# Attention scores on row tiles, with both images of a pair issued together

## The reference

```python
t = t + _L2_attn_ref(_ln_t(t), ...)   # 8 heads of 16, causal window of 64 keys
t = t + _L2_ffn_ref(_ln_t(t), ...)    # y = x @ binarized weight + bias; y = round(clip(y, -1, 1) * 7) / 7
t = t + _L3_attn_ref(_ln_t(t), ...)   # 8 heads of 16, causal
t = t + _L3_ffn_ref(_ln_t(t), ...)    # 8 experts, the best two of softmax(x @ W_router)
# each attention: scores = q @ k.T / 4; masked softmax; out = probs @ v; out @ W_o
```

## Time and profile before

| | |
|---|---|
| median of 3 runs | 270.75 us (270.49 to 271.74) |
| profiled execution, its own time | 271.7 us |
| its span, first to last instruction | 269.9 us |
| granted TensorE clock over the span | 1.000 |
| busy PE, DVE, ACT, POOL | 93%, 79%, 64%, 31% |
| phases of attention | 43.6 to 71.6, to 105.3, to 138.6, to 171.8 |
| experts | from 171.8 |

### The profile page before, as it was taken

How to read it: one execution, slowest core, us unless ns; L and a number is a source line. 1 busy time by engine, 2 the same in 40 slices (tenths; PEclk the granted TensorE clock), 3 DMA queues, 4 the chain that set the end, 5 groups by cost and what they waited for, 6 DMA issues and landing times.

```text
span 269.9 us, 4613 instructions
## 1 busy us (share of the span) xinstructions
PE 251.7 (93%) x1545; PEld 184.6 (68%) x1547; DVE 212.7 (79%) x542; ACT 172.6 (64%) x490; POOL 83.8 (31%) x151
## 2 busy tenths in 40 slices
PE   7999879699998998989999899999899999999994
PEld 2777557465776566666576666788678878888883
DVE  3675669965599797997979957397699969599985
ACT  2276344698676856768667697675485587567760
POOL 5100104988894762946724220000400000000000
PEclk9999999999999999999999999999999999999999
DMA  7800000014222020000000000041101000531101
GB/s 219 323 2 2 0 1 0 0 29 130 80 78 79 8 73 2 0 2 0 0 5 0 0 2 2 24 134 43 38 32 47 2 0 0 170 99 48 39 0 39
DMA packets 9318, 11.84 MB, mean 44 GB/s; under 512 B 704, under 2 KB 5952, under 8 KB 9168
## 3 DMA queue, kind: packets, MB, share of 16 engines
q1 hardware_dynamic: 8864, 11.23, 13.7%
q10 hardware_dynamic: 432, 0.33, 0.4%
HBM read 11.00 MB, written 0.56 MB: 43 GB/s over the span
## 4 chain that ended last, share of the span: by engine, by line
PE 57%; DVE 30%; ACT 6%; issue 4%; POOL 2%; DMA 1%; DVEq 0%; SPq 0%; ACTq 0%
PE bank L717 5%; PE bank L729 5%; PE bank L693 5%; PE bank L665 5%; DVE negmax L1083 5%; PE bank L959 4%; PE bank L960 4%; PE bank L962 4%; PE bank L947 4%; PE bank L949 3%; PE bank L948 3%; DVE probT L1142 3%; DVE hlo L1337 2%; DVE ht L1049 2%; DVE stats L1035 2%
## 5 line engine op out<-in xcount | busy, mean ns | idle before, releaser
L479 ACT ACTIVATE prob<-bank,negmax 128x256 f32<-128x256 f32 (+1 forms) x128 | 52.5, 425 | 17.1 <-DVE negmax L1083 16.7
L606 ACT ACTIVATE hb<-bank,pk 128x512 f32<-128x512 f32 x64 | 42.8, 708 | 17.8 <-PE bank L949 17.8
L1337 DVE TENSOR_TENSOR hlo<-hb,hhi 128x512 fp32r<-128x512 f32 x64 | 42.7, 689 | 11.9 <-ACT hhi L609 10.8
L1083 DVE TENSOR_REDUCE negmax<-bank 128x2 f32<-128x512 f32 (+1 forms) x48 | 32.6, 686 | 13.1 <-PE bank L699 12.6
L717 PE MATMUL bank<-pk,prob 128*128 128x128 f32 x192 | 29.4, 277 | 2.2 <-ACT prob L479 1.7
L344 POOL TENSOR_TENSOR rstd<-ve,neghalf 128x2 f32<-128x2 f32 x16 | 11.5, 729 | 58.4 <-DVE ve L1044 58.4
L479 ACT ACTIVATION_READ_ACCUMULATOR prob<-bank,negmax 128x1 f32 x128 | 26.6, 208 | 0.0
L717 PEld LDWEIGHTS bank<-pk,prob 128*128 128x128 f32 x192 | 22.0, 142 | 6.3 <-ACT prob L479 3.6
L729 PE MATMUL bank<-probT,vh 128*32 128x128 f32 x384 | 25.8, 280 | 0.1
L947 PE MATMUL bank<-xhi,w_hi 128*128 128x512 f32 x64 | 25.4, 397 | 0.2
L959 PE MATMUL bank<-hhi,w_hi 128*128 128x512 f32 x64 | 25.3, 395 | 0.0
(11 more groups left out here) (149 smaller groups left out, 503.3 us busy)
## 6 DMA issues: line engine op xcount, KB each, us to landing
w_raw<-w SPq DMA_DIRECT2D x16, 256.0 KB, 3.1
comb_b<-routes SPq DMA_DIRECT2D x16, 256.0 KB, 3.4
pk<-packed SPq DMA_DIRECT2D x1, 1408.0 KB, 8.6
pk<-packed SPq DMA_DIRECT2D x1, 560.0 KB, 5.6
xs<-x SPq DMA_DIRECT2D x3, 128.0 KB, 2.7
out<-acc SPq DMA_DIRECT2D x3, 128.0 KB, 1.7
xs<-x ACTq DMA_DIRECT2D x1, 128.0 KB, 2.9
out<-acc ACTq DMA_DIRECT2D x1, 128.0 KB, 1.7
```

Source lines behind the costliest of these rows:

```text
L479: last = nc.scalar.activation(prob[n][:, u % 2, i * width:(i + 1) * width], lane[n][u % 2][:, i * width:(i + 1) * width], ACT.Exp, bias=ne ...
L606: nc.scalar.activation(hb[blk % 2][:, j, :], h_bank[j][:, :], ACT.Relu, bias=bias).then_inc(h_ready, 1)
L1083: V.tensor_reduce(negmax[n][:, unit_query(u), heads[0]:heads[-1] + 1], lane[n][u % 2][:, :].rearrange("q (h k) -> q h k", h=len(heads)), A ...
L1337: V.tensor_tensor(hlo[blk % 2][:, j, :], hb[blk % 2][:, j, :], hhi[blk % 2][:, j, :].bitcast(F32), ALU.subtract).then_inc(hlo_ready, 1)
```

## The change

The scores no longer use masked keys. The projection's weights are laid out by rows (`by_rows`), so that each 32 partitions hold one head of a group g: 16 rows that become the keys' high part and 16 that become the low part. One multiplication with the column `rowsign` gives both parts. A head's scores are then a product on one row tile of 32 partitions, 128 or 256 keys wide, for the queries' low and high parts: four products in a wide unit and eight in a narrow one, per image, where two of 512 columns stood. The mask goes first and starts the bank.

A wide unit takes one row tile (two heads), a narrow one two. Row tiles of one image write the same bank, so PE waits in between for its own last product (`rows_done`). Image 1 takes another row tile than image 0, and from step 1 on both images' products alternate. Heads are dealt by `head_of`, so that the heads of a unit and its pair lie on different column tiles in `mix`, where both images' products alternate too.

The order is new as well. PE: scores of both, side work, mix of both, transposes of both. ACT: exponentials of the first, copy of the first's turned probabilities, exponentials of the second; DVE copies the second's. DVE: both maxima, bias sums between them, that copy, then both quantizations, statistics and norms. `NEXT_STEP` is 5 for 4. Between phases the first image is turned and projected, then comes the last mix, then the second image. `hlo` changes places in SBUF with the space that attention's outputs take.

```diff
+def head_of(g, r):
+    return HG * g + (r + 2 * g) % HG
...
-        kM = each("kM", [128, HEADS, T], F32R, n=2, scope=attention_memory)
...
-        STATS_STEP, NORM_STEP, TURN_STEP, PRODUCT_STEP, NEXT_STEP = 1, 2, 3, 4, 4
+        STATS_STEP, NORM_STEP, TURN_STEP, PRODUCT_STEP, NEXT_STEP = 1, 2, 3, 4, 5
...
-        SCORE_BANKS = ((1, range(0, 2)), (0, range(0, 4)), (1, range(2, 4)),
-                       (0, range(4, 8)), (1, range(4, 6)), (1, range(6, 8)))
-        SECOND_HALF = next(u for u, (_, heads) in enumerate(SCORE_BANKS) if heads[0] >= HG)
+        SCORE_UNITS = ((1, (0,)), (0, (0, 1)), (1, (1,)), (0, (2, 3)), (1, (2,)), (1, (3,)))
         def unit_query(u):
-            return SCORE_BANKS[u][0]
-        def unit_heads(u):
-            return SCORE_BANKS[u][1]
...
+            return SCORE_UNITS[u][0]
+        def unit_rows(n, u):
+            return sorted(r ^ (n % 2) for r in SCORE_UNITS[u][1])
+        def unit_heads(n, u):
+            return [head_of(g, r) for r in unit_rows(n, u) for g in range(2)]
+        def unit_maxima(n, u):
+            rows = unit_rows(n, u)
+            of_rows = negmax[n][:, unit_query(u), :].rearrange("q (a b) -> q b a", b=2)
+            return of_rows[:, rows[0] % 2:rows[0] % 2 + len(rows), slice(0, 4, 3) if rows[0] < 2 else slice(1, 3)]
...
-                for i, h in enumerate(unit_heads(u)):
+                for i, h in enumerate(unit_heads(n, u)):
...
-                    for n in ns:
...
+                    if aside and u == TURN_STEP:
+                        for n in ns:
+                            turned(aside, other(n))
+                    if u < UNITS:
+                        exps(a, ns[0], u)
+                    if u >= 1:
+                        probs_turned(a, ns[0], u - 1)
+                    if u < UNITS:
+                        exps(a, ns[1], u)
...
-            def scores(a, n, u):
+            def masked(a, n, u):
                 if u == 0:
                     pe.wait_ge(q_lo_ready, a * B + n + 1)
-                    pe.wait_ge((kM_ready, kM_act_ready)[n % 2], (a * B + n) // 2 + 1)
-                if u == SECOND_HALF:
-                    pe.wait_ge(kM2_ready, a * B + n + 1)
                 if u == 1:
                     pe.wait_ge(av_ready, a * B + n + 1)
                 if u >= 2:
                     pe.wait_ge(exp_done[n], a * UNITS + u - 1)
-                width = unit_width(u)
...
+                i, width = unit_query(u), unit_width(u)
                 seen = slice(128, T) if (a, i) == (1, 1) else slice(0, width)
-                dst = dst[:, :].rearrange("q (h k) -> q h k", k=width)[:, :, seen]
+                dst = lane[n][u % 2][:, :].rearrange("q (h k) -> q h k", k=width)[:, :, seen]
                 mask = A_MASK[a][i][:, seen].unsqueeze(1).to_broadcast(list(dst.shape))
-                mm(dst, ident_bf, mask, start=False, stop=True, skip_group_check=True).then_inc(s_full[n], 1)
+                mm(dst, ident_bf, mask, start=True, stop=False, skip_group_check=True)
+            def scores(a, ns, u):
+                for n in ns:
+                    masked(a, n, u)
+                i, width = unit_query(u), unit_width(u)
+                row_count = len(SCORE_UNITS[u][1])
+                for at in range(row_count):
+                    for n in ns:
+                        if at:
+                            pe.wait_ge(rows_done[n], 2 * a + (u + 1) // 2)
+                    for part in (q_hi, q_lo):
+                        for g in range(2):
+                            for n in ns:
+                                place = at if n % 2 == 0 else row_count - 1 - at
+                                r = unit_rows(n, u)[place]
+                                rows = slice(HP * r, HP * r + HP)
+                                col = (2 * place + g) * width
+                                last = mm(lane[n][u % 2][:, col:col + width],
+                                          part[n % 2][rows, g, i * 128:(i + 1) * 128],
+                                          k_parts[n % 2][rows, g, 0:width],
+                                          start=False, stop=(part is q_lo), tile_position=(HP * r, 0),
+                                          skip_group_check=True)
+                                if (part, g) == (q_lo, 1):
+                                    last.then_inc(s_full[n] if at == row_count - 1 else rows_done[n], 1)
...
-            def mix(a, n, u):
-                pe.wait_ge(pT_ready[n], a * UNITS + u + 1)
+            def mix(a, ns, u):
+                for n in ns:
+                    pe.wait_ge(pT_ready[n], a * UNITS + u + 1)
                 key_tiles = unit_width(u) // 128
-                for kt in range(key_tiles):
...
+                products = [(kt, i, n) for kt in range(key_tiles) for i in range(4 // key_tiles) for n in ns]
+                if key_tiles == 1:
+                    products.sort(key=lambda product: product[2])
+                for kt, i, n in products:
+                    h = unit_heads(n, u)[i]
+                    g, r = divmod(h, HG)
+                    col = (2 * g + unit_query(u)) * 128
+                    at = (i * key_tiles + kt) * 128
+                    last = mm(lane[n][3][HP * r:HP * r + HP, col:col + 128], vh[n][:, kt, h, :],
+                              probT[n][:, u % 2, at:at + 128],
+                              start=(kt == 0), stop=(kt == key_tiles - 1), tile_position=(0, HP * r))
+                    if u == UNITS - 1 and (kt, i) == (key_tiles - 1, 4 // key_tiles - 1):
+                        last.then_inc(av_full, 1)
...
             def unit_step(a, ns, u, aside, before=None):
+                if u == 0:
+                    for n in ns:
+                        scores(a, (n,), u)
+                elif u < UNITS:
+                    scores(a, ns, u)
                 if u == 1 and before is not None:
                     for n in ns:
-                        scores(a, n, u)
-                    for n in ns:
                         project_out(before, other(n))
+                for job, at in ((turn, TURN_STEP), (product, PRODUCT_STEP)):
+                    if aside and u == at:
+                        for n in ns:
+                            pe.wait_ge(pT_ready[n], a * UNITS + at - 1)
+                            job(aside, other(n))
+                if u >= 2:
+                    mix(a, ns, u - 2)
+                if 1 <= u <= UNITS:
                     for n in ns:
                         turn_probs(a, n, u - 1, aside)
-                    return
...
+                    first, second = following[1]
                     if p >= 1:
-                        for n in following[1]:
...
+                        turn(2, first)
+                    project(following[0], first)
+                    unit_step(a, ns, UNITS + 1, ASIDE[p])
+                    if p >= 1:
+                        turn(2, second)
+                    project(following[0], second)
+                else:
+                    unit_step(a, ns, UNITS + 1, ASIDE[p])
             def turn_routes(h):
...
-                low = k_parts[n % 2][64:128, :, :]
-                V.tensor_tensor(low, lane[n][1][64:128, :].rearrange("r (g t) -> r g t", g=2), low.bitcast(F32),
-                                ALU.subtract).then_inc(k_parts_ready, 1)
+                parts = k_parts[n % 2]
+                V.scalar_tensor_tensor(parts[:, :, :], lane[n][1][:, :].rearrange("r (g t) -> r g t", g=2),
+                                       const("rowsign", 0, 1), parts[:, :, :].bitcast(F32), ALU.mult, ALU.subtract
+                                       ).then_inc(k_parts_ready, 1)
...
             def units(a, ns, aside, a_before):
                 before = [other(n) for n in ns]
                 for u in range(UNITS + 1):
-                    if u == 1 and a_before is not None:
-                        for n in ns:
+                    for n in ns:
+                        if 0 < u < UNITS:
                             largest(a, n, u)
-                        for n in before:
-                            add_attention(a_before, n)
-                    for n in ns:
                         if u == PRODUCT_STEP and aside == 1:
                             dve.wait_ge(ffn_full, other(n) + 1)
                             V.tensor_tensor(fy[n % 2][:, :, :], tiles(lane[n][2][:, T:2 * T]), tiles(const("fb")),
                                             ALU.add).then_inc(ffn_copied, 1)
-                            quantize(other(n))
                         if u == PRODUCT_STEP and aside == 3:
                             logits(other(n))
-                        if 0 < u < UNITS and not (u == 1 and a_before is not None):
...
+                    if u == 1 and a_before is not None:
+                        for n in before:
+                            add_attention(a_before, n)
+                    if u >= 1:
+                        dve.wait_ge(pT_full[ns[1]], a * UNITS + u)
```

(42 more changed lines are left out.)

72 lines of the change are left out of this document (11 added, 61 removed).

## The result

The changed kernel took 286.81 us (median of four executions, 283.94 to 289.83), the kernel before beside it 271.22 (270.49 to 271.74). The ratio is 1.055, with a 95% interval of 1.051 to 1.059. The forecast was 271.6 with a range of 266 to 277, so it missed by 15.2 us, and the time lies 10 us outside the range. The profiled execution is the longest of the four (289.83), and part of its excess over the others is clock: its mean granted clock is 0.929, theirs 0.940 to 0.958.

A forecast was written before the change was run, and what follows sets the result against it. The prediction took PE (93% busy, 57% of the chain) as the bound, with DVE often ending last. PE work -10.4 and waits +11.3 gave +0.9 on the 270.75 us median: 271.6, range 266 to 277.

The forecast's parts named there:

- PE's own work at the full clock: Four attention phases: scores, mixing and transposes together change PE's work by -2.6 us a phase, -10.4 in all.
- waits of PE, net: Four attention phases: 19.1 us of new PE waits less 7.8 gone, net +11.3.
- PE idle before the mix of unit 4: Phases 1 and 2: PE waits 3.2 and 3.4 us at mix(4), ended by an ACT copy of turned probabilities.
- Unit 5's maxima: DVE, phase 1: they start only behind both quantizations, 7.45 us after the start of unit 4's masks.
- The turn behind: First image's turn for the next layer's norm: PE waits 2.4 us for 0.6 before.
- ACT's hT: Four turns each followed by their own project: PE waits 0.6 us for it, with no second turn to cover.
- Phase 3: New PE waits of 3.9 us: best_experts ahead of unit 5's maxima 1.9, and smaller ones.
- The first phase: The first of the four attention phases becomes 2 us shorter, the next two no shorter.
- turns of the side norm: PE's 3.4 us of waits for norms of the side work counted as gone, those norms being a step later.
- B: Rival, faster: smaller waits, second quantization not slowed, narrow rounds at the lower end (0.06 for 128 keys); 266.5 us, chance 0.30.
- C: Rival, slower: narrow fp32r score products cost 0.22 a round and not 0.12; 276 us, chance 0.20.
- D: Rival, slower: row tiles don't run beside each other or don't hide their loads; 277 to 280 us, chance 0.10.

The follow-up runs named there:

- e2: The changed kernel with 60 idle full-array products in PE's long waits (last-but-one mix, next norm's turn, projections): 280.77 us, ratio 1.037.
- e10: The changed kernel with DVE's second quantization, phases 1 and 2, behind unit 5's maxima and the copy of unit 4's turned probabilities: 281.64 us, ratio 1.031.
- e8: e2 plus three and four idle products before the side norm's turns of phases 1 and 2: 278.16 us, ratio 1.026.
- e1: The kernel before with stretches of one kind of product each (full array, row tiles, column tiles) behind its end; two-tile 256-column round 0.123 us, no total given.
- e3: The changed kernel with the same score products on all 128 rows, no row tiles, waits left in, scores summed over heads: 285.06 us, ratio 1.053.
- e9: The changed kernel with the edits of e2 and e3 together, waits filled and no row tiles: 279.17 us, ratio 1.031.
- e7: e6 plus eight idle products before the first side norm turn of phases 1 and 2: 267.83 us, ratio 0.988 to the kernel before.
- e6: The kernel before with only both images' mixes alternating on four column tiles, masked keys and full-row scores kept: 269.06 us, ratio 0.995.
- e5: e2 plus two idle products before masks of units 0, 1 and 3 and three before each side turn, 126 in all: 285.72 us, ratio 1.053.

## Why the prediction was wrong

**The step that failed** is its sum, "-10.4 + 11.3 = +0.9". Both terms were priced at the full clock, from rows of an execution that never leaves it, and there was no term for the clock that the change itself would cost. Such a term belongs there: the same text forecast PE idle for 3 us in two phases and 32-row products four times narrower than the full array, and took the rate from the rows of an unbroken stream. With the phases of the profiled execution the account is:

| term | forecast | measured | from |
|---|---|---|---|
| PE's own work at the full clock | -10.4 | -10.8 | 108.1 (e2) against 118.9 |
| waits of PE, net | +11.3 | +13.3 | 21.8 against 8.5 |
| half clock | 0 | +16.3 | 124.4 busy against 108.1 |
| four phases | +0.9 | +18.8 | 146.2 against 127.3 |

The third term is a remainder. Halving the 34.7 us of busy time in the six stretches gives 17.3, an upper bound, since latencies don't all double. The profiled execution is the one with the lowest clock; the medians differ by 15.6, so in a usual execution the clock took some 13.

**Right, by its own signs.** PE idle before the mix of unit 4, ended by ACT's copy: 2.90 and 3.06 for 3.2 and 3.4. Unit 5's maxima start 7.4 behind unit 4's masks (93.58 and 100.97 in the changed kernel) for 7.45. The turn behind: 2.17 twice for 2.4. ACT's hT: 0.47 for 0.6. Phase 3: 1.75 and 0.87 for 1.9 and the smaller ones. A pair's wide rows, 61.51 to 62.33, take 0.82 and in another unit 0.67, for 0.69; narrow rows 1.43 (58.05 to 59.48) for 1.47; the mix 0.57 for 0.62. e10 shows the cause of the first wait, the order in DVE's queue.

**Off in size.** The first phase became 1.2 us shorter, not 2; e2 has it at 26.4, 1.7 shorter, without its fall at 52. The net of waits was 2.0 too low, and one term of it was wrong: it counted 3.4 us of waits at the turns of the side norm as gone. In phase 3 they are gone, but in phases 1 and 2 the turns still wait, 1.21 and 1.46 where it was 1.07 and 1.23. Phase 2, before and then after:

```profile
121.66 0.41 PE L642 MATMUL bank<-pk,ht 128*128 128x128 f32 x2 [1.23 <-DVE ht L1049]
...
130.88 0.59 PE L635 MATMUL bank<-pk,ht 128*128 128x128 f32 x2 [0.79 <-DVE ht L1064]
132.14 0.66 PE L635 MATMUL bank<-pk,ht 128*128 128x128 f32 x2 [0.67 <-DVE ht L1064]
```

With the measured waits and without the clock the phases would have stood at +2.5, about 273 to 274 us (an estimate): slower, but inside the range. No run realizes that version. The nearest is e8 at 277.3 to 279.2, which carries 74 idle products, some outside any wait, and still some falls; its profiled execution less half of its 10.3 us at the low clock would be 274.0.

**Rivals.** B is out by both of its conditions: a narrow round is 0.111 and not 0.06, and unit 5's maxima start 7.4 behind unit 4's masks and not less than 6. C and D are out (e1). That the change is slower, which the forecast had at 0.42, came by another mechanism than C's or D's: products too thin and waits too long for TensorE to hold its clock. Nothing in the earlier trace rows shows a fall, and that was the trap: the kernel before has a clock of 0.997 to 1.000 in all its executions but one (0.994, at 271.88 us), and its longest wait in the phases is 1.33 us, so a forecast from its rows can't see what happens once PE pauses for longer.

What stays open is how the two causes add. Some spots fall in one execution and not in another (52.4 and 80 did in the changed kernel and in e8, not in e2), so the share of each of them can't be told from single profiles. By medians, filling waits gives 6.0, full rows 1.8 (within the spread), and both 7.6, though full rows cost PE 6.2 of busy time. Full rows also fill some of the short waits, so e3 and e9 don't part thin products from a less busy PE as cleanly as e1 does.

## What to carry to other kernels

Where TensorE runs at its full clock, price a change twice: once by durations, and once by what it does to the clock, since every busy us at half the clock can cost up to half a us more than the work it holds. A gain for TensorE (thinner products, fewer of them) that ends in waits can lose more than it saves; filling such a wait with idle products that end before the wait would cost nothing in e7 (the filled turn starts at 117.51, the unfilled one of e6 at 117.73), and e5 shows the price when they don't fit. Try a bundle's parts alone: here the alternating mix without row tiles keeps the gain (e7).

## What the runs showed of the hardware

- Within a stretch of fp32r products on one 32-row tile of 256 columns, back to back with PE 100% busy, the clock fell to 1.2 GHz, and so it did with two row tiles at 128 columns; two tiles at 256 columns, four row tiles and two or four column tiles held 2.4 GHz (e1). The Trainium skill (TensorE: Matmul & The Clock Gate, Part 1) names idle gaps of PE as what lowers the clock; the falls behind waits agree in kind (e3, e6), but these two stretches show a fall with no gap at all.
- The clock was at half behind a single wait of 1.99 us in e6 and of 1.93 in e7, both in kernels without a row tile. Another of 1.82 us (85.02) in e6 had no fall behind it, nor had those of up to 1.33 in the kernel before.
- The fp32r row-tile round is 0.12 us for two tiles of 256 columns and 0.11 for two of 128. At half the clock a single tile's products lie 0.213 apart for 0.120, and a round of two tiles at 128 columns takes 0.213 for 0.111 (e1).
- The same kernel's executions spread more once the clock falls: 0.5% before, 2.1% for the changed kernel, 1.9% in e10.
